# An expert layer's first tile taken early in float32, and its last tile in two halves

## The reference, cut to what matters

```python
x = x + _L0_ffn_ref(_L0_cond_ref(x, cond_128, ...), ...)
x = x + _L1_ffn_ref(_L1_cond_ref(x, cond_128, ...), ...)

def _L1_ffn_ref(x, gate_w, gate_b, expert_w, expert_b):
    xf = x.reshape(-1, x.shape[-1])                 # 2048 x 1024
    gates = softmax(xf @ gate_w.T + gate_b)
    selected = argmax(gates, axis=-1)               # one of 8 experts
    out = zeros
    for j in range(8):
        yj = xf @ expert_w[j].T + expert_b[j]       # 1024 x 1024 each
        out = out + where((selected == j)[:, None], yj, 0.0)
    return out.reshape(...)
```

## Time and profile before

| | us |
|---|---|
| timed executions | 1385.14, 1387.16, 1389.26 (median 1387.16) |
| profiled execution, own time | 1384.71 |
| its span | 1383.10 |
| TensorE busy | 1369.2 (99%) |
| VectorE busy | 1113.5 (81%) |
| ScalarE busy | 774.5 (56%) |
| GpSimd busy | 225.6 (16%) |

### The profile page before, as it was taken

One profiled execution on the slowest core, in us unless ns is written; L12 is line 12 of the kernel. 1 busy time (PEld: TensorE's weight loads), 2 busy tenths in 40 slices (PEclk: granted clock), 3 DMA queues, 4 the chain that ended last, 5 costly groups with the idle time before them and its releaser, 6 DMA issues.

```text
span 1383.1 us, 20668 instructions
## 1 busy us (share of the span) xinstructions
PE 1369.2 (99%) x6816; PEld 1125.6 (81%) x6816; DVE 1113.5 (81%) x1127; ACT 774.5 (56%) x872; POOL 225.6 (16%) x251
## 2 busy tenths in 40 slices
PE   9999999999999999999999999999999899999998
PEld 8987888888888888888888888888765688888887
DVE  7879887878878788787887887878643799999997
ACT  6665554545454545445464554555216677777774
POOL 0120000001000000000000000000013256645653
PEclk9999999999999999999999999999999999999999
DMA  7863756587874779666886759885588786978952
GB/s 243 343 248 137 270 205 244 188 290 250 276 272 176 273 252 288 238 241 225 282 250 245 261 195 298 255 286 214 198 303 283 238 256 153 375 198 290 352 173 54
DMA packets 105108, 339.50 MB, mean 245 GB/s; under 512 B 15716, under 2 KB 23404, under 8 KB 105036
## 3 DMA queue, kind: packets, MB, share of 16 engines
q1 hardware_dynamic: 79122, 257.93, 50.1%
q0 software_dynamic: 25376, 80.24, 21.5%
q10 hardware_dynamic: 546, 0.50, 0.1%
HBM read 303.49 MB, written 46.14 MB: 253 GB/s over the span
## 4 chain that ended last, share of the span: by engine, by line
PE 94%; DVE 3%; issue 1%; ACT 1%; DMA 0%; POOL 0%; DVEq 0%; SPq 0%; ACTq 0%; POOLq 0%
PE pair L1281 27%; PE pair L1282 27%; PE pair L1283 27%; PE pair L1350 4%; PE pair L1618 1%; DVE wf L873 1%; PE pair L1530 1%; PE pair L1520 1%; PE pair L1464 1%; PE pair L1382 1%; PE pair L1365 1%; PE pair L1542 1%; PE pair L1343 1%; PE pair L1290 1%; PE pair L1419 0%
## 5 line engine op out<-in xcount | busy, mean ns | idle before, releaser
L873 DVE TENSOR_TENSOR wf<-wf,term 128x1024 f32<-128x1024 f32 x308 | 376.5, 1222 | 62.7 <-ACT term L618 48.3
L618 ACT ACTIVATE term<-codes 128x1024 f32<-128x1024 int32 x308 | 320.6, 1055 | 137.7 <-DVE wf L873 137.7
L1281 PE MATMUL pair<-wh,hh 128*128 128x512 f32 x672 | 263.3, 392 | 1.6 <-DVE acc L937 1.3
L1282 PE MATMUL pair<-wl,hh 128*128 128x512 f32 x672 | 262.0, 390 | 0.0
L1283 PE MATMUL pair<-wh,hl 128*128 128x512 f32 x672 | 262.0, 390 | 0.0
L1281 PE MATMUL pair<-ring,wh 128*128 128x512 f32 x624 | 242.9, 389 | 0.0
L1282 PE MATMUL pair<-ring,wh 128*128 128x512 f32 x624 | 242.9, 389 | 0.0
L1283 PE MATMUL pair<-ring,wl 128*128 128x512 f32 x624 | 242.7, 389 | 0.0
L943 DVE TENSOR_TENSOR acc<-acc,pair 128x1024 f32<-128x1024 f32 x160 | 194.5, 1216 | 46.2 <-PE pair L1283 40.2
L807 ACT ACTIVATE whr<-wraw 128x1024 fp32r x176 | 181.1, 1057 | 63.9 <-PE pair L1283 49.8
L1255 DVE TENSOR_TENSOR wlr<-wraw,whr 128x1024 fp32r<-128x1024 f32 x176 | 203.4, 1215 | 2.1 <-ACT whr L807 1.9
(11 more groups left out here) (202 smaller groups left out, 1557.3 us busy)
## 6 DMA issues: line engine op xcount, KB each, us to landing
ring<-x_parts SPq DMA_DIRECT2D x320, 512.0 KB, 6.5
wraw<-exp_w SPq DMA_DIRECT2D x64, 512.0 KB, 10.5
x_parts<-stage POOLq DMA_DIRECT2D x24, 512.0 KB, 7.0
xg<-exp_b POOLq DMA_DIRECT2D x23, 512.0 KB, 7.9
codes<-codes_up SPq DMA_DIRECT2D x22, 512.0 KB, 7.1
codes<-codes_dn SPq DMA_DIRECT2D x22, 512.0 KB, 6.8
am<-am_dn SPq DMA_DIRECT2D x22, 512.0 KB, 4.1
acc<-x_nat POOLq DMA_DIRECT2D x16, 512.0 KB, 5.5
```

What stands on the lines that cost most here:

```text
L618: return nc.scalar.activation(out, codes[:, n % 2], ACT.Relu, scale=scale, bias=-scale * bend)
L873: nc.vector.tensor_tensor(whole(n), whole(n), term[:, e % 2], op).then_inc(term_added, 1)
L1281: mm(ps, ah, bh, start=first, stop=False)
L1282: mm(ps, ah, bl, start=False, stop=False)
```

## The change

*The early tile.* The first of the 23 tiles is no longer the first of expert 0, but the first 128 rows of the fullest expert, as counted over the first eight tiles of rows. To know it early the batches become 0 to 7, 8 to 10 and 11 to 15. TensorE counts the experts of the first half (`counted`), VectorE picks the fullest (`lead`) and makes row numbers (`lead_columns`, `rows_of_lead`) from a table of the first half alone (`placed(0, 8)` once more, into other columns of bank 7). SyncE loads this expert's weights in whole into the odd buffer (`load_lead`), before expert 1's, which now wait for the buffer slice by slice. GpSimd gathers the rows ahead of the store of z's last tile. All later places of this expert shift by 128 rows. `lead_product` multiplies the turned rows with the unsplit weights in plain float32, 16 products 128 x 512, and has the second half of `placed` after kt 1 and the transposes of the next tile after kt 5. The five calls of `spin` between the gating loop and the first product are gone.

*The last tile.* `last_product` runs all slices for the first 512 columns and then all for the others; VectorE adds, and GpSimd scatters, each half by itself.

```diff
-BATCHES = (0, 6, 11, TILES)
+BATCHES = (0, TILES // 2, 11, TILES)
...
-                        sp.wait_ge(z_ready, 2 * TILES if e else 4 * kt + 2)
+                        sp.wait_ge(*((chunk_mm, kt + 1) if e else (z_ready, min(4 * kt + 2, 26))))
...
+            def load_lead():
+
+                sp.wait_ge(lead_ready, 1)
+                first = sp.value_load(eti[0:1, 0:1], min_val=0, max_val=E - 1)
+                for kt in range(KT):
+                    sp.dma_start(wraw[:, 1, kt], exp_w[bass.ds(first, 1), :, kt].rearrange("a p n -> p (a n)")
+                                 ).then_inc(wraw_in[1][kt], 16)
+
             load_expert(0)
+            load_lead()
             load_expert(1)
...
             for t in range(TILES):
+                if t == TILES - 1:
+
+                    for k in range(ZB):
+                        pool.wait_ge(z_stored[k], 32 * (TILES // 2) // ZB)
+                    pool.wait_ge(lead_rows_ready, 1)
+                    pool.sem_inc(zidx_ready, 1)
+                    pool.indirect_dma_start(zg[:, 0], None, z_dram[0:N // 2], bass.IndirectOffsetOnAxis(lead_rows[:], 0),
+                                            bounds_check=half_row, oob_is_err=False).then_inc(zg_in[0], 16)
...
-            gather_z(0, 0)
+            gather_z(0, 1)
             pool.wait_ge(columns_ready, 1)
-            for s in range(1, 3):
-                gather_z(0, s)
+            gather_z(0, 2)
             gather_x(0, 0)
             gather_x(0, 1)
...
+            def first_low():
+                for kt in range(KT):
+                    dve.wait_ge(whr_ready, KT + kt + 1)
+                    nc.vector.tensor_tensor(wlr[:, kt], wraw[:, 0, kt], whr[:, kt], ALU.subtract).then_inc(wlr_ready, 1)
+                    if kt == 3:
+                        z_low(0, 1)
+                add_rows(0, 0)
...
+            def lead_product():
+
+                for kt in range(KT):
+                    if kt == 0:
+                        pe.wait_ge(half_copied, 1)
+                    elif kt == KT // 2:
+                        pe.wait_ge(zth_ready, 1)
+                    pe.wait_ge(wraw_in[1][kt], 16)
+                    for h in range(2):
+                        ins = mm(bank[2 + h], lead_turn[:, kt], wraw[:, 1, kt, h * 512:(h + 1) * 512],
+                                 start=kt == 0, stop=kt == KT - 1)
+                    ins.then_inc(chunk_mm, 1)
+                    if kt == 1:
+                        placed(TILES // 2, TILES)
+                    elif kt == 5:
+                        pe.wait_ge(table_ready, 1)
+                        rows_transposed(0, 1)
+
+            def last_product(i, s):
+
+                pe.wait_ge(ztl_ready, i * 4 + s + 1)
+                pe.wait_ge(y_ready, i * 4 + s - 1)
+                for h in range(2):
+                    d = slice(h * 512, (h + 1) * 512)
+                    for kt in range(KT):
+                        if h == 0:
+                            pe.wait_ge(wlr_ready, i * 32 + KT * (s + 1) + kt + 1)
+                        ins = three(bank[2 * (1 - s % 2) + h], zth[:, s % 2, kt], ztl[:, s % 2, kt], whr[:, kt, d], wlr[:, kt, d],
+                                    kt == 0, kt == KT - 1)
+                    ins.then_inc(half_mm_last, 1)
...
             rows_transposed(0, 0)
-            spin(bank[1], 5)
+            placed(0, TILES // 2)
+            ranks(2)
+            totals(1)
+            lead_product()
```

More of the change, by code:

```diff
@@ L528, in gather_z @@
                 rows = zidx[:, s % 4:s % 4 + 1]
-                if isinstance(i, int) and 4 * i + s == 0:
-                    rows = table[:, 0:1]
+                if isinstance(i, int) and 4 * i + s == 1:
+                    rows = table[:, 1:2]
                     pool.sem_inc(zidx_ready, 1)
@@ L571, in tile @@
                     add_bias(i, s + 1)
-                scatter(i, s)
-            gather_z(0, 0)
+                if left > 1:
+                    scatter(i, s)
+                else:
+                    scatter_last(i, s)
+            gather_z(0, 1)
             pool.wait_ge(columns_ready, 1)
-            for s in range(1, 3):
-                gather_z(0, s)
+            gather_z(0, 2)
             gather_x(0, 0)
@@ L817, in _ @@
                 for s in range(4):
-                    if not (isinstance(i, int) and i == s == 0):
+                    if not (isinstance(i, int) and i == 0 and s < 2):
                         convert_high(i, s)
@@ L1142, in _ @@
                     picked(t - 2)
-                if t == TILES - 1:
-                    marked(6, 7)
+                if t == 9:
+                    choose(0)
+                    count_seen(0)
+                elif t == 10:
+                    lead()
+                elif t == 11:
+                    digits(0)
+                    more_digits(0)
+                    marked(0, 2)
+                elif t == 12:
+                    choose(1)
+                    count_seen(1)
+                elif t == 13:
+                    marked(6, 8)
+                elif t == 15:
+                    digits(1)
                 if t > 0:
@@ L1223, in _ @@
             for b in range(2):
[L1224 to L1239 removed]
+                nc.vector.tensor_scalar(loads[:, b, 1:], loaded[:, b], 8.0, 16.0, ALU.mult, ALU.add).then_inc(tiles_ready, 1)
             def z_low(i, s):
@@ L1565, in ranks, with placed, counted @@
                 ins.then_inc(rank_mm, 1)
-            def placed(first, last):
+            def placed(first, last, at=P, end=TILES):
                 for t in range(first, last):
                     pe.wait_ge(row_ready, 2 * (t + 1))
-                    ins = mm(bank[7][:, P:P + SC], atrow[:, t], atcol[:, t], start=t == 0, stop=t == TILES - 1)
-                if last == TILES:
-                    ins.then_inc(slot_mm, 1)
+                    ins = mm(bank[7][:, at:at + SC], atrow[:, t], atcol[:, t], start=t == 0, stop=t == end - 1)
+                if last == end:
+                    ins.then_inc(slot_mm if end == TILES else lead_mm, 1)
+            def counted():
+                pe.wait_ge(seen_ready, 1)
+                mm(bank[7][:, 3 * P:3 * P + E], ones_b[:], seen[:, 0], start=True, stop=True).then_inc(count_mm, 1)
             def totals(b):
@@ L1589, in _ @@
                     z_transposed(t)
+                if t == 10:
+                    ranks(0)
+                    counted()
                 if 1 < t < TILES:
@@ L1643, in _ @@
             rows_transposed(0, 0)
-            spin(bank[1], 5)
+            placed(0, TILES // 2)
+            ranks(2)
+            totals(1)
+            lead_product()
             for i in rounds(pe, NS // 4):
                 for s in range(4):
-                    product(i, s)
-            for s in range(NS % 4):
+                    if not (isinstance(i, int) and i == s == 0):
+                        product(i, s)
+            for s in range(NS % 4 - 1):
                 product(NS // 4, s)
+            last_product(NS // 4, NS % 4 - 1)
 def layouts(x, cond_128, fside_S_0, L0_cond_weight, L0_cond_c_weight, L0_ffn_w_up_codes, L0_ffn_w_up_absmax,
```

187 lines of the change are left out of this document (105 added, 82 removed).

## The result

| | before | after |
|---|---|---|
| median, us | 1387.13 (20 runs) | 1392.26 (20 runs; 1391.93 over 18 of them, 1387.04 to 1399.00) |
| ratio, 95% interval | | 1.0041 (1.0030 to 1.0053) |
| profiled execution: own time, span | 1384.71, 1383.1 | 1396.05, 1394.5 |

Two executions of after took 3672 and 6351 us; they are left out of the ratio and of the 18, and no profile shows what slowed them.

What follows compares the result with a forecast made beforehand. TensorE, 94% of the chain, bounds the kernel. Third product 1130.35 to 1130.8, less 0.55 at the end, turns span 1383.1 into 1383.0: no change. Forecast 1386.6 us, the mean of four executions; range 1380.0 to 1391.2.

Steps and rivals of the forecast that it cites:

- open stretch: TensorE between the gating loop's end at about 1091 and the first product: some 13 us open, taking a whole tile.
- when the first gather is issued: GpSimd issues the gather of the early tile's rows at 1088.9, 1.08 us after its row numbers.
- the late logits: VectorE's small operations in the gating loop: 0.7 us added for logits that come late, bounded by 0 and 2.
- the half clock of the first product: First 3.9 us of the early tile's product at half speed: kt 0 and 1 take 5.5 us, ends 3.6 and 7.1.
- the addition behind the last matmul: VectorE's last addition covers 512 instead of 1024 columns: 0.69 us against 1.22.
- I take 6.2, near that median.: Landing time of the first gather beside queued expert loads: 6.2 us, range 4.4 to 10.5, landed at 1095.1.
- T: Time when the table of slots is written: 1098.83 before, forecast 1104.0, 5.2 us later.
- I take 7.0 [...] Then 0.6 us to the issue and 5.3 for the bias: T + 21.0.: First tile's x gather, issued at T + 8.1, then its bias: landed at T + 21.0, ends T + 17.4 and T + 24.5.
- From there [...] nothing is won back.: From the third product on, VectorE needs 11.34 us a tile, TensorE 11.8: nothing more late, nothing won back.
- TensorE stands still for about 4 us ahead of it: TensorE idles about 4 us ahead of the third product, which starts at T + 26.8 = 1130.8 against 1130.35 before.
- The end: Last tile in halves: 0.55 us gained behind the last matmul, with ends 0 and 0.8.
- The slower rival: First gather lands after 10.5 us, holds up the routing: table 1109.9, 1392.4 us; measurably slower from table 1108.3; 13%.

Runs made afterwards that it cites:

- early tile alone: The kernel after without the halves of the last tile (one product, one add, one store there): 1391.87 us, 1.0041 to before.
- next loads held: The kernel after with the next expert's eight weight loads issued only when the first tile's bias has landed: 1385.85 us, 0.9995 to before.
- table first: The kernel after with last ranks, totals and all table products on TensorE ahead of the first tile's transposes: 1388.39 us, 1.0007 to before.
- first add later: The kernel after with VectorE's first addition behind the seventh conversion for the third product, not ahead of the first: 1388.77 us, 1.0009 to before.

## Why the prediction was wrong

- *What bounds the kernel, where the open stretch lies, when the first gather is issued* (1088.9 against 1088.5), the late logits, the half clock of the first product (kt 0 and 1: 5.5 forecast, 4.8 measured in after and 4.0 with the early tile alone), the addition behind the last matmul: right.
- *"I take 6.2, near that median."* Too short by 2.2 to 2.6 us. The loads that stood in SyncE's queue were named and not priced; without six of them it was 5.8. T came 1.1 to 2.3 us late by it. The next tile's gather was put at 5.9 us and took 6.3 and 7.2, so that the second product came late too (T + 11.5 and T + 14.0, not T + 11.0); the third does not depend on it, since ztl came later still.
- *"I take 7.0 [...] Then 0.6 us to the issue and 5.3 for the bias: T + 21.0."* This is the step that failed. The order of waits was right and these terms were 4 to 5 us short: the bias lands 17.1 to 18.2 us behind the issue of the x gather, not 12.9. The x gather with the step to the bias's issue took 9.2 to 10.4 us and not 7.6, the bias 7.8 to 7.9 and not 5.3. With the next loads held the sum is 11.9. So expert 1's loads, "strung out", load the DMA engines for just this stretch. The 5.3 was a single transfer, not the median of its line. 0.9 us of it came back, as the x gather was issued at T + 7.2 and not T + 8.1.
- *"From there [...] nothing is won back."* Right, but something is lost: behind the wait the clock is at 1.2 GHz, and the stretch is 2.1 to 2.2 us longer in the two profiles. Whether these count in the median stays open. The prediction had a half clock at its first gap and none at its second.
- *"TensorE stands still for about 4 us ahead of it"*: 3.8 and 7.5 in two executions. *The end*: 0.55 forecast, 1.15 measured, as GpSimd's gap shrank as well; in a median it could not be told.
- The slower rival had a late gather hold up the routing, table at 1109.9. The table was at 1105 to 1106, below its 1108.3. Its time (1392.4) is the one measured, by luck: its mechanism is not what happened. With 8.0 us for the x gather and 7.9, the median of its line in the kernel before, for the bias, my own sum would have been T + 30.4 = 1134.4 and the forecast some 1390.
- Profiles and medians: the first part of a run falls on levels some 3.4 us apart, and the later turns hold 0 to 7 us of waits. One profile is not a median of either. The profiles put the early tile's loss at 7.0 us, the ratio at 5.7.

## What to carry to other kernels

Work that waits for a transfer must not stand, on its engine, ahead of work that doesn't and that a busier engine needs; here moving the additions was worth 2.4 us in the kernel before. With them moved, the table first and TensorE's gaps filled, the change, which cost 5 us by itself, was worth 6. When something is pulled forward, price the transfers behind it by the median of their line, with the loads that run beside them in the new order. Hold back loads that nobody needs yet while short transfers are waited for. And try filling TensorE's idle gaps ahead of dense work: it paid 3 to 4 us ahead of the first transposes, and nothing that could be told ahead of the third product.

## What the runs showed of the hardware

- A gather of 512 KB landed in 8.2 to 8.8 us beside eight loads of 512 KB (414 GB/s), and in 5.8 to 6.1 us with six of them held back.
- GpSimd's issue of a gather takes 1.0 to 1.2 us as a rule, but in kernels with the old place of the add two to five of them took 5.8 to 5.9 us each. Where every add was moved only one issue was long, that of a scatter (5.4 or 6.5 us). Whether the long issues are a cause of the late biases or come with them was not tested.
- Behind TensorE's gaps of 2.7 us (first add later), 3.1 (table first) and 7.5 (after) the granted clock of the third product's first microseconds was 0.50, in the second of them only from its second microsecond on; behind one of 2.6 us (next loads held) it stayed at 1.00. At 0.50 the matmuls of 512 columns follow each other every 0.43 us and not 0.23. The clock was back at 1.00 after 2.9 us (first add later), 5.6 (after) or 6.2 (early tile alone) of dense work, so that one value from one place does not carry over.
